# Six and five edge groups in turn per message step, ring positions by register, 24 groups behind the last step

## The reference

```python
xn = layernorm(x)
# gnn: mean of xn[src] over the edges into each node
agg = segment_sum(xn[src], dst, N) / maximum(segment_sum(1, dst, N), 1)
g = relu(agg @ W_l.T + b_l + xn @ W_r.T) + xn
# mix: linear attention over all nodes, 8 heads, then an MLP
Q, K, v = elu(xn @ Wq) + 1, elu(xn @ Wk) + 1, (xn @ Wv) / N
KV = einsum("shd,shv->hdv", K, v)                    # a sum over all nodes
msg = N * einsum("lhd,hdv->lhv", Q, KV) / (Q . K.sum(0) + 1e-6)
msg = layernorm(msg @ Wm, g1, b1)
h = relu(concat([xn, msg]) @ W1) @ W2
x = x + g + (xn + layernorm(h, g2, b2))
# ffn: on the 6249 nodes with the highest score, after a layernorm of x
w = layernorm(x) @ wr + br
y[top_k(w)] = (gelu(layernorm(x)[top_k(w)] @ w1 + b1) @ w2 + b2) * w[top_k(w)]
x = x + y + layernorm(x)
```

## Time and profile before

| | |
|---|---|
| median of three runs | 2594.31 us |
| the profiled execution, its span | 2591.4 us, 2589.7 us |
| mean granted TensorE clock | 0.937 |
| PE busy (matmuls) | 2200.0 us, 85% |
| PEld busy (weight loads) | 1826.8 us, 71% |
| DVE (VectorE) busy | 1316.4 us, 51% |
| ACT (ScalarE) busy | 902.0 us, 35% |
| POOL (GpSimd) busy | 1696.3 us, 66% |

### The profile page before, as it was taken

The page is one execution under the profiler, slowest core; times in us unless marked ns, Lnnn a source line. Parts: engine busy times, 40 slices in busy tenths (PEclk is TensorE's granted clock), DMA queues, the critical chain, the costliest instruction groups (busy, mean ns, idle before and its releaser), DMA issues.

```text
span 2589.7 us, 48874 instructions
## 1 busy us (share of the span) xinstructions
PE 2200.0 (85%) x13352; PEld 1826.8 (71%) x13353; DVE 1316.4 (51%) x3156; ACT 902.0 (35%) x1949; POOL 1696.3 (66%) x1817
## 2 busy tenths in 40 slices
PE   1399999997888888888888888888999899589998
PEld 1287777775667667666676666767777678379998
DVE  8644444443444344454444445544555589844444
ACT  8433333331222222222222222222232258444554
POOL 3577777777777777777777777777777511045553
PEclk6699999998998999999999999999999999689999
DMA  9766666664555555555555555555555489711111
GB/s 332 231 194 187 183 185 180 187 179 149 153 162 156 154 154 165 153 162 156 154 154 152 159 159 162 156 154 154 158 169 158 147 258 295 264 34 46 45 43 35
DMA packets 218372, 419.29 MB, mean 162 GB/s; under 512 B 40579, under 2 KB 107141, under 8 KB 218286
## 3 DMA queue, kind: packets, MB, share of 16 engines
q0 software_dynamic: 88352, 243.57, 33.0%
q1 hardware_dynamic: 129118, 173.95, 20.0%
q10 hardware_dynamic: 816, 0.79, 0.1%
HBM read 321.63 MB, written 96.52 MB: 161 GB/s over the span
## 4 chain that ended last, share of the span: by engine, by line
POOL 37%; PE 37%; issue 14%; DVE 5%; DMA 4%; ACT 1%; DVEq 1%; POOLq 0%; SPq 0%; ACTq 0%
POOL gath_raw L713 37%; PE ps L1779 11%; PE ps L1626 4%; PE ps L1547 3%; PE ps L1719 3%; PE ps L1549 3%; PE ps L1592 3%; DMA gath_raw<-xtab,srcI 3%; PE ps L1636 2%; PE ps L1532 2%; DVE stats L791 1%; PE ps L1674 1%; PE ps L1644 1%; DVE gath_raw L810 1%; PE ps L1715 1%
## 5 line engine op out<-in xcount | busy, mean ns | idle before, releaser
L713 POOL DMA_INDIRECT gath_raw<-xtab,srcI x1563 | 1484.0, 949 | 476.5 <-issue 464.0
L1547 PE MATMUL ps<-gath_raw,onehot 128*128 128x256 f16 x1956 | 477.4, 282 | 205.0 <-DMA gath_raw<-xtab,srcI 115.5
L887 DVE SCALAR_TENSOR_TENSOR onehot<-ps,blkbase,dstF 128x512 f32 x489 | 354.0, 745 | 255.3 <-issue 170.8
L1549 PE MATMUL ps<-gath_raw,onehot 128*128 128x257 f16 x1956 | 478.4, 282 | 0.0
L1547 PEld LDWEIGHTS ps<-gath_raw,onehot 128*128 x1956 | 194.7, 100 | 290.3 <-issue 260.6
L1626 PE MATMUL ps<-work,w_s 128*128 128x256 f32 x1568 | 394.6, 408 | 2.5 <-issue 1.7
L1626 PEld LDWEIGHTS ps<-work,w_s 128*128 128x128 f32 x1568 | 312.5, 205 | 49.8 <-issue 2.7
L961 DVE BATCH_NORM_STATS2 stats<-ps 128x6 f32<-128x256 f32 x196 | 74.4, 422 | 456.7 <-PE ps L1674 452.1
L1779 PE MATMUL ps<-split_raw 128*128 128x256 f32 x2376 | 293.0, 285 | 1.7 <-DVE split_raw L1226 1.5
L1779 PEld LDWEIGHTS ps<-split_raw 128*128 128x128 f32 x2376 | 288.1, 193 | 2.4 <-issue 1.9
L1360 ACT ACTIVATE work<-ps 128x512 f32<-128x512 f32 x98 | 58.5, 597 | 499.5 <-PE ps L1626 499.5
(11 more groups left out here) (215 smaller groups left out, 2990.5 us busy)
## 6 DMA issues: line engine op xcount, KB each, us to landing
work<-x_in SPq DMA_DIRECT2D x98, 256.0 KB
lin_raw<-lin_d POOLq DMA_DIRECT2D x49, 512.0 KB, 4.6
gath_raw<-xtab,srcI POOLq DMA_INDIRECT x1563
agg<-x_in SPq DMA_DIRECT2D x14, 896.0 KB, 7.9
xt_d<-work SPq DMA_DIRECT2D x49, 256.0 KB, 4.3
q_d<-work SPq DMA_DIRECT2D x49, 256.0 KB, 2.5
work<-q_d SPq DMA_DIRECT2D x49, 256.0 KB, 3.3
work<-xt_d SPq DMA_DIRECT2D x49, 256.0 KB, 3.1
```

The source lines that it names most:

```text
L713: e.indirect_dma_start(out=gath[:, TPG * s + t, 0:2 * D], out_offset=None, in_=xtab[:, :], in_offset=bass.IndirectOffsetOnAxis(ap=srcI[:, ...
L887: v.scalar_tensor_tensor(out=onehots[:, ds(p % OHN * TPG, TPG), :], in0=ps[:, columns:columns + 1, 0:P].to_broadcast(shape), scalar=blkbas ...
L1547: t.matmul(ps[:, ds(BG + k % 2, 1), 0:D], oh, gath[:, r, 0:D], start=False, stop=False, skip_group_check=True)
L1549: last = t.matmul(ps[:, ds(BG + k % 2, 1), 0:AGW], oh, gath[:, r, D:2 * D + 1], start=False, stop=q == TPG - 1, skip_group_check=True)
```

## The change

The message steps take six and five groups in turn: 25 steps of six and 24 of five are 270 groups, from group 98 (`MAT`) to group 367. The last 24 (`TAIL`, from `TAILAT` = 368) follow the last step: six written out between its remaining products, 12 in a loop of six, and the last six written out. All steps but the first two and the last are now in the looped body of two.

Eleven groups pass in two steps, and the ring has six places, so a group's ring place in the looped steps is `(m_first(s, j) + t) % RING` of a register, for PE's address of the rows; GpSimd's side is written out and keeps constants. Rows are counted on one semaphore for each of the eleven positions in two steps: `rows_in0` to `rows_in5` and the new `rows_m0` to `rows_m4`.

```diff
-KG, MG = 2, 6
-TAIL = 7
-MFULL = NSUP - TAIL
+KG = 2
+MPAIR = (6, 5)
+MAT = KG * NSUP
+TAILAT = MAT + sum(MPAIR[i % 2] for i in range(NSUP))
+TAIL = NG - TAILAT
...
+        def m_first(s, j):
+            return MAT + sum(MPAIR) * j + sum(MPAIR[:s])
+        def landing(g):
+            p = (g - MAT) % sum(MPAIR)
+            return rows_m[p - RING] if MAT <= g < TAILAT and p >= RING else rows_in[g % RING]
+        def landed(g):
+            return TPG * len([o for o in range(g + 1) if landing(o) is landing(g)])
...
# GpSimd, every gather
-                    ).then_inc(rows_in[s], 16)
+                    ).then_inc(landing(g), 16)
...
# PE
-            def seg(slot, use, first, more, end):
+            def seg(rows_of, lists, slot, first, more, end):
-                padded = max(0, (use * RING + slot + 1) * TPG - (NG * TPG - GPAD)) if isinstance(use, int) else 0
-                landed = 16 * TPG * use + 16 * (TPG - min(TPG, padded))
+                row = slot * TPG if isinstance(slot, int) else e.snap(slot * TPG)
+                landed_at = 16 * lists
...
-                    e.wait_ge(rows_in[slot], landed)
+                    e.wait_ge(rows_of, landed_at)
-                        r = TPG * slot + q
+                        r = row + q if isinstance(row, int) else ds(row + q, 1)
...
-                one = gath[:, TPG * slot, 2 * D:2 * D + 1]
+                one = gath[:, 0, 2 * D:2 * D + 1]
...
+            def m_seg(s, j, t, span):
+                g = m_first(s, 0) + t
+                seg(landing(g), landed(g) + TPG * j, (m_first(s, j) + t) % RING, *span)
...
-            steps(e, m_body, MFULL, 2)
-            for i in range(MFULL, NSUP):
-                m_body(i, i % 2, i // 2)
+            steps(e, m_body, NSUP, 2)
-            for k, g in enumerate(tail):
-                seg(*place(g), *seg_values(e, mybir.EngineType.PE, g, 1)[0])
+            for k in range(RING):
+                seg(landing(TAILAT + k), landed(TAILAT + k), (TAILAT + k) % RING, *seg_values(e, mybir.EngineType.PE, TAILAT + k, 1)[0])
...
+            with e.Fori(1, TAIL // RING - 1) as j:
+                spans = seg_values(e, mybir.EngineType.PE, TAILAT + RING * j, RING)
+                for k in range(RING):
+                    seg(landing(TAILAT + k), landed(TAILAT + k) + TPG * j, (TAILAT + k) % RING, *spans[k])
+            spans = seg_values(e, mybir.EngineType.PE, NG - RING, RING)
+            for k in range(RING):
+                missing = min(TPG, max(0, TPG * (k + 1) - (TPG * RING - GPAD)))
+                seg(landing(NG - RING + k), landed(NG - RING + k) - missing, (TAILAT + k) % RING, *spans[k])
```

VectorE's sums end with one full `add_before` and one plain addition, without clearing the bank behind it; its key loop leaves the last steps to be written out (`tail` of `steps()`: four more than before); and its split of the feed-forward part's first weights waits for GpSimd's second staging copy instead of a semaphore of its own that GpSimd raised behind the first gathers:

```diff
-            steps(e, k_body, NSUP, 3)
+            steps(e, k_body, NSUP, 3, 3)
...
-            e.wait_ge(grp_used, NG)
-            add_before()
-            e.reg_mov(before, held)
-            e.reg_mov(since, pair)
-            add_before()
-            k = e.snap(full)
-            e.wait_ge(seg_added, k + 2)
+            add_before()
+            e.wait_ge(grp_used, NG)
+            b, k = e.snap(held), e.snap(full)
+            v.tensor_tensor(agg[:, ds(b, 1), :], agg[:, ds(b, 1), :], ps[:, ds(BG + k % 2, 1), 0:AGW], ALU.add).then_inc(sum_read, 1)
+            e.wait_ge(sum_read, k + 1)
...
-                if not past(i, 1):
-                    e.sem_inc(f_sent, 1)
...
-            e.wait_ge(f_sent, 1)
+            e.wait_ge(fstage[1], 1)
```

More of the change, by code:

```diff
@@ L276, in build @@
         rows_in = [sem(f"rows_in{i}") for i in range(RING)]
-        ones_set = sem("ones_set")
+        rows_m = [sem(f"rows_m{i}") for i in range(sum(MPAIR) - RING)]
         iota_ps = sem("iota_ps")
@@ L281, in build @@
         bnd_tab = sem("bnd_tab")
-        k_x_in = [sem(f"k_x_in{i}") for i in range(3)]
+        x_rows_in = [sem(f"x_rows_in{i}") for i in range(3)]
         k_xn = sem("k_xn")
@@ L567, in _ @@
             for i in range(2):
-                e.dma_start(kx[i], rows(x, 2 * i)).then_inc(k_x_in[i], 16)
+                e.dma_start(kx[i], rows(x, 2 * i)).then_inc(x_rows_in[i], 16)
             e.wait_ge(bnd_out, 16)
@@ L578, in k_io @@
                         e.wait_ge(k_xn, i)
[L579 removed]
+                    e.dma_start(kx[(s + 2) % 3], rows(x, 2 * i + 4)).then_inc(x_rows_in[(s + 2) % 3], 16)
                 e.wait_ge(k_xnT, i + 1)
@@ L591, in m_load @@
             def m_load(i, s):
-                e.dma_start(mx[s], rows(x, 2 * i)).then_inc(m_x_in[s], 16)
+                e.dma_start(mx[s], rows(x, 2 * i)).then_inc(x_rows_in[s], 16)
                 e.dma_start(flat(mq[s]), turned(q_d, i)).then_inc(m_q_in[s], 16)
@@ L1052, in _ @@
                     m_end(i, i % 2, ch + 3)
-            e.wait_ge(grp_used, NG)
-            add_before()
-            e.reg_mov(before, held)
-            e.reg_mov(since, pair)
-            add_before()
-            k = e.snap(full)
-            e.wait_ge(seg_added, k + 2)
+            with e.Fori(1, TAIL // RING) as j:
+                g0 = TAILAT + RING * j
+                spans = seg_values(e, mybir.EngineType.DVE, g0, RING)
+                for t in range(RING):
+                    seg(g0 + t, BA, *spans[t])
+            add_before()
+            e.wait_ge(grp_used, NG)
+            b, k = e.snap(held), e.snap(full)
+            v.tensor_tensor(agg[:, ds(b, 1), :], agg[:, ds(b, 1), :], ps[:, ds(BG + k % 2, 1), 0:AGW], ALU.add).then_inc(sum_read, 1)
+            e.wait_ge(sum_read, k + 1)
             base = own_m + 10 * NSUP
@@ L1397, in m_body @@
                 last.then_inc(m_ynT, 1)
-                e.wait_ge(m_x_in[s], 16 * j + 16)
+                e.wait_ge(x_rows_in[s], 16 * (len(range(s, NSUP, 3)) + j + 1))
                 if past(i, 2):
@@ L1678, in m_body @@
                     l_product(i - 1, 1 - s)
[L1679 removed]
+                m_seg(s, j, 3, spans[3])
                 if past(i, 1):
                     m_mlp_out(i - 1)
[L1682 removed]
+                m_seg(s, j, 4, spans[4])
                 e.wait_ge(m_yn, i + 1)
                 transposes(BB, myn).then_inc(m_yT_ps, 1)
[L1685 to L1689 removed]
+                for k in range(5, MPAIR[s]):
+                    m_seg(s, j, k, spans[k])
+            steps(e, m_body, NSUP, 2)
             i = NSUP - 1
[L1692 to L1693 removed]
+            for k in range(RING):
+                seg(landing(TAILAT + k), landed(TAILAT + k), (TAILAT + k) % RING, *seg_values(e, mybir.EngineType.PE, TAILAT + k, 1)[0])
                 if k < 2:
```

73 lines of the change are left out of this document (24 added, 49 removed).

## The result

The changed kernel takes 2680.13 us, the median of four runs (2677.92 to 2681.03), against 2594.65 for the kernel before: slower by the factor 1.033 (95% interval 1.0318 to 1.0342). The forecast was 2652 us with TensorE as the new bound.

A forecast was written before the change was run, and what follows sets the result against it. GpSimd's gathers bound the kernel until 2055 us; TensorE would become the bound. On the profiled 2591.4 us, + 93 - 22 - 13 = + 58 gives 2649, plus 2.9 to the median: 2652 us, own range 2605 to 2700.

The forecast's parts named there:

- The bound turns from GpSimd's gathers to PE's sequencer: Message steps: PE needs 29.5 us a step where the gathers take 27.6, so TensorE becomes the bound; chance 0.76.
- 1.0 us a cold pair: Looped message steps: register ring place adds eight sequencer instructions and longer formulas to a pair (eight matmuls), 1.0 us where PE waits.
- 2.95 cold pairs a step: Pairs where PE waits for its sequencer: groups 1 and 2, half the sixth's; 2.95 in the mean, 2.9 us a step.
- 0.2 us a step for spells of lower clock: Message steps on PE: allowance of 0.2 us a step for the lower-clock spells taken out of the base need.
- 29.5 us a step on PE: Mean message step on PE: 26.4 us, plus 2.9 for cold pairs and 0.2 for lower clock, against 27.6 of gathers.
- + 93 - 22 = + 71 us: GpSimd's last gather: 1.9 us a step over 49 steps is 93 later, of which the ring absorbs 22 once.
- - 13 us for the shorter end: From last gather to ScalarE's first L1419: 10.2 us instead of 23.2, with 24 groups behind the last step, saving 13.
- The key loop and the moved wait, 0: VectorE's peeled key loop, covered by gathers, and its weight split's wait moved to the second staging copy: each taken as 0.
- Shared semaphores: the same waits on other counters, but one moves: Semaphore changes leave all waits the same except that of VectorE's first weight split; between - 0.7 and + 1.3 us, taken as 0.
- Sequencer hidden, 2581: Rival, message steps: a cold pair costs 0.5 us, the ring absorbs the excess, only the end changes: 2581 us; chance 0.13.
- The clock, 2725: Rival, message steps: gaps between matmuls bring TensorE's lower clock, one spell every step, 1.5 us x 49 more: 2725 us; chance 0.08.
- the trace shows no such swing: Argument against the clock rival: in the five-group steps PE stands still 0.38 and 0.35 us ahead of pairs, clock 1.00.

The follow-up runs named there:

- own_rows_2: Changed kernel with each gather counted on the semaphore of its group's position in two steps, not on the rotating rows_in[g % RING]: 2634.35 us, 1.0155 of the kernel before.
- own_const_2: Changed kernel with semaphores by position and constant ring places (PE's message loop written as a body of twelve steps): 2578.29 us, 0.9943 of the kernel before.
- before_reg_2: Kernel before with the ring place in looped message steps worked out from a register, giving the changed kernel's code for a pair: 2641.43 us, 1.0186.
- own_light: own_rows_2 with a group's four rows taken as one slice from the register, five more sequencer instructions a pair instead of eight: 2590.24 us, 0.9987 of the kernel before.

## Why the prediction was right, and where it was wrong

*The bound turns from GpSimd's gathers to PE's sequencer*: right. Undoing the register code takes 56 us away (own_rows_2 to own_const_2), doing it alone adds 48 (before_reg_2).

*1.0 us a cold pair*: 2.50 us apart, against 1.40 before and 1.47 in own_const_2, so 1.0 to 1.1: right. *2.95 cold pairs a step*: in the trace of own_rows_2 the matmuls stand more than 0.15 us apart in 2.5 of 7.15 pairs a step, all of group 1 and two thirds of groups 2 and 6, so that term was some 0.4 us too large. *0.2 us a step for spells of lower clock*: too small, see the rivals. *29.5 us a step on PE*: 29.1 in own_rows_2. Over 49 steps that 0.4 is 20 us, so the term + 93 - 22 = + 71 us at the last gather was too large: with the register code and without the rotation it is 2110.1 - 2054.0 = + 56.

*- 13 us for the shorter end*: - 14.4 in the changed kernel (23.2 to 8.8), - 14.2 in own_const_2.

*The key loop and the moved wait, 0*: the last stage is 316.8 us from the first staging copy to the end, against 317.7; in own_rows_2, own_light and own_const_2, which share its code, it is 316.3, 316.3 and 317.5, so the difference is no more than their scatter. With + 56 and - 14 in place of + 71 and - 13 the prediction's sum is 2636 us; own_rows_2, which is the change without the error that follows, measures 2634.

*"Shared semaphores: the same waits on other counters, but one moves"*: wrong, and the section on the change says the same ("rows are counted on one semaphore for each of the eleven positions"). Five of eleven positions have one; the other six rotate. This term, taken at 0, is + 44 us at the last gather (2154.3 - 2110.1) and + 46 in the median. The profile of before couldn't show it, but the diff did: `g % RING` on one side, a constant index on the other. So 2652 lies within 28 us of the measured time partly by luck: a term that was 15 us too large stood beside one of 46 that was missing.

*The rivals.* Sequencer hidden, 2581: that is what own_const_2 shows for a kernel without its work, 2578. The clock, 2725, is out as the whole of the loss, but not as a part of it. By stretch, the changed kernel, own_rows_2 and own_light have 0.94, 0.96 and 0.98 (the third number from the end), where the kernel before has 0.95:

```profile
596.00:1945.00 1349.00, 1179.88 (x6357) 906.39 (x6357) 601.31 (x1487) 338.78 (x803) 958.25 (x1006) 0.94 0.50 150
```

```profile
596.00:1945.00 1349.00, 1208.54 (x6556) 926.18 (x6556) 620.94 (x1529) 348.04 (x824) 983.51 (x1036) 0.96 0.52 154
```

```profile
596.00:1945.00 1349.00, 1196.19 (x6776) 943.19 (x6776) 640.75 (x1578) 358.24 (x849) 1014.47 (x1067) 0.98 0.53 159
```

A mean near that of before doesn't say that the register code leaves the clock alone. In the kernel before PE waits for 2 to 4 us at a time in 25 of the 40 looped steps, which is where the earlier trace rows has its matmuls at the lower level. In the 46 looped steps of own_rows_2 PE never stands still for more than 1.6 us, and still the granted clock is below 1.00 in 24 of them; in own_light, with three instructions less on a pair and one wait of 2.2 us, it is in 12. In the changed kernel it falls behind the long waits (the pair at 833.08 us has matmuls of 0.39 us), but also at 1425.86 in the timeline above, in a step whose longest idle time is 1.11 us. What such a spell costs is read from the same step (37, counted from 0) of two kernels with the same code for a pair. PE's idle times in it are the same in both, 0.9 us the longest. First the changed kernel, then own_rows_2:

```profile
1689.59:1720.76 31.17, 27.34 (x142) 20.65 (x141) 13.58 (x34) 6.56 (x17) 22.40 (x24) 0.95 0.49 150
```

```profile
1650.29:1679.77 29.48, 25.65 (x143) 19.47 (x142) 13.56 (x34) 6.56 (x17) 22.43 (x24) 1.00 0.53 158
```

That is 1.7 us; in step 38 a spell costs nothing (29.32 against 29.31 us). As an estimate from these figures, between nothing and some 24 x 1.7 = 41 of the 56 us between own_rows_2 and own_const_2, and between nothing and some 12 x 1.7 = 20 of the 44 us between own_rows_2 and own_light, go through the clock; no run parts it from the sequencer's own time. So the mechanism of the rival (the gaps between matmuls bring the lower level) is at work, but in half of the steps and for some 0.9 us a step at most, where the rival had 1.5 and the forecast 0.2. The Trainium skill (TensorE: Matmul & The Clock Gate, A second HAM failure mode: psum-queue depth-cycling) tells of a kernel whose short idle spells between groups of matmuls made the clock swing; the trace of own_rows_2 agrees with it, and the prediction's "the trace shows no such swing" held for the five steps that it looked at, where the places were constant and PE stood still for 0.5 us at most ahead of a pair.

## What to carry to other kernels

Where an index of a ring becomes a register, look at the code between matmuls: eight more sequencer instructions in each pair, most of them of 32 to 74 ns, were worth 56 us here, part of it perhaps through the clock. Unrolling until the index is constant again brought all of it back, slicing once 44 us. When semaphores are handed out by a formula, write both sides' index for a few turns of the loop side by side; a wait for a later event is no error that any output shows, only time, and the same formula gave other positions a wait for an earlier event, which only the order of PE's work made harmless. A wait of a consumer for data while its ring is full is the sign of it in a timeline.

## What was not expected of the hardware

On the chips where the kernel before takes 3050 us, single instructions of the sequencers take up to 0.7 us. PE's register work of one line (duration ns min/median/max), of the same kernel, first where it takes 2578 us, then where it takes 3044, followed there by GpSimd's gathers:

```profile
L1536 PEldq FUSED_REGOPS  x2445: 46/46/167, 114.6 to 2058.4; - x189
```

```profile
L1536 PEldq FUSED_REGOPS  x2445: 3/46/709, 112.0 to 2536.4; - x189
...
L702 POOL DMA_INDIRECT gath_raw<-xtab,srcI x1563: 940/946/1396, 95.2 to 2525.0; - x196
...
  issue: 443.0, 1357
  remote: 314.7, 122
```

The gathers themselves take 946 ns on both. The 315 us ahead of them in 122 places end with an event that the profile can't name. What causes it stays open; the order of the kernels is the same on both kinds of chip, and the ratios differ by up to 0.7%.
